# Third attention and late expert stages of a four-layer attention and expert network: first tiles, weight loads and the first group placed elsewhere

## The reference

```python
x = x + _L1_ffn_ref(_layernorm(x), ...)          # experts 1: top 2 of 8, capacity 256
# layer 2: 16 heads of 64, keys and values from the 128 context rows and the 128 latents
xn   = _layernorm(ctx, ln1_w, ln1_b);  latn = _layernorm(layernorm(x), ln2_w, ln2_b)
q, kv = latn @ Wq, concat([xn, latn]) @ Wkv
x = x + heads_attention(q, k, v) @ Wo
# experts 2 (top 2 of 8, gated, hidden 256); experts 3 (top 1 of 8, gelu, hidden 512)
hidden = silu(gate_out) * up_out;  expert_out = hidden @ down_w[e]
x = x + _L3_xattn_ref(...)                       # attention 3: one head of 128
h = gelu(x @ w1[e] + b1[e]);  y = h @ w2[e] + b2[e]
```

## Time and profile before

| what | us |
| --- | --- |
| median of 3 runs | 1901.37 |
| their range | 1900.53 to 1907.52 |
| profiled execution | 1909.33 |
| its span | 1907.6 |
| busy: PE, PEld, DVE, ACT, POOL | 1488.1, 1337.0, 1164.3, 824.9, 763.8 |
| mean granted TensorE clock | 0.852 of 2.4 GHz |

### The profile page before, as it was taken

How to read it: one execution, slowest core, us unless ns; L and a number is a source line. 1 busy time by engine, 2 the same in 40 slices (tenths; PEclk the granted TensorE clock), 3 DMA queues, 4 the chain that set the end, 5 groups by cost and what they waited for, 6 DMA issues and landing times. The chain is left out here.

```text
span 1907.6 us, 36653 instructions
## 1 busy us (share of the span) xinstructions
PE 1488.1 (78%) x10440; PEld 1337.0 (70%) x10441; DVE 1164.3 (61%) x3672; ACT 824.9 (43%) x2537; POOL 763.8 (40%) x757
## 2 busy tenths in 40 slices
PE   6776999425677639999999999999994898446394
PEld 4555899313466539999999999999993787224294
DVE  4556344217867337787778777777775455574244
ACT  4343455201222126666666666666661232313152
POOL 2011543560000535454747474756454355011442
PEclk8786899756666769999999999999997899766597
DMA  9002322110011230000000000000001522200223
GB/s 190 1 0 70 118 65 59 47 48 1 1 45 45 57 97 13 1 12 1 24 1 22 0 22 1 21 0 11 3 10 34 149 72 65 89 9 14 63 64 114
DMA packets 91845, 79.06 MB, mean 41 GB/s; under 512 B 16820, under 2 KB 78871, under 8 KB 91623
## 3 DMA queue, kind: packets, MB, share of 16 engines
q1 hardware_dynamic: 70712, 44.92, 9.0%
q0 software_dynamic: 11936, 24.52, 4.4%
q10 hardware_dynamic: 9104, 8.53, 1.5%
HBM read 51.36 MB, written 27.60 MB: 41 GB/s over the span
## 5 line engine op out<-in xcount | busy, mean ns | idle before, releaser
L1838 POOL TENSOR_TENSOR paired_rows<-paired_rows,rinv 128x1024 f32<-128x1024 f32 x128 | 242.3, 1893 | 284.6 <-DVE rinv L2123 281.6
L2002 ACT ACTIVATE paired_rows<-psum_banks,neg_max 128x256 f32<-128x256 f32 x512 | 237.4, 490 | 0.2
L2114 DVE TENSOR_TENSOR probs_turned_lo<-psum_banks,probs_turned_hi 128x512 fp32r<-128x512 f32 x256 | 175.5, 686 | 96.4 <-ACT probs_turned_hi L1984 82.8
L1888 PE MATMUL psum_banks<-y_turned_parts,queries_hi 128*128 128x256 f32 x1024 | 199.9, 293 | 3.0 <-DVEq L1739 3.0
L1923 PE MATMUL psum_banks<-probs_turned_hi,y_rows 128*128 128x512 f32 x512 | 192.0, 416 | 0.4 <-issue 0.4
L1984 ACT CAST probs_turned_hi<-psum_banks 128x512 fp32r<-128x512 f32 x256 | 151.1, 590 | 57.5 <-PE psum_banks L1872 55.1
L1872 PE MATMUL psum_banks<-ident,paired_rows 128*128 128x128 f32 x1024 | 154.9, 274 | 7.8 <-DVEq L1739 4.4
L1888 PEld LDWEIGHTS psum_banks<-y_turned_parts,queries_hi 128*128 128x128 f32 x1024 | 158.0, 191 | 3.5 <-issue 3.5
L2128 DVE TENSOR_REDUCE neg_max<-psum_banks 128x4 f32<-128x1024 f32 x128 | 155.9, 1218 | 6.5 <-PE psum_banks L1888 3.5
L1984 ACT CAST queries_hi<-psum_banks 128x512 fp32r<-128x512 f32 x128 | 75.0, 586 | 172.5 <-PE psum_banks L1911 167.6
L1888 PE MATMUL psum_banks<-y_turned_parts,queries_lo 128*128 128x256 f32 x512 | 144.5, 282 | 0.0
(11 more groups left out here) (717 smaller groups left out, 3386.2 us busy)
## 6 DMA issues: line engine op xcount, KB each, us to landing
tile_rows__<-rows_by_expert SPq DMA_DIRECT2D x71, 64.5 KB
expert_rows<-expert_rows_sb SPq DMA_DIRECT2D x71, 64.0 KB, 1.5
normed_rows_dram<-paired_rows SPq DMA_DIRECT2D x2, 2048.0 KB, 8.9
staged_pairs<-expert_rows SPq DMA_DIRECT2D x8, 512.0 KB
paired_rows<-expert_rows SPq DMA_DIRECT2D x8, 512.0 KB, 6.0
tile_rows___<-rows_by_expert SPq DMA_DIRECT2D x39, 64.5 KB
x_rows<-in_x_dram SPq DMA_DIRECT2D x8, 256.0 KB, 5.3
expert_w_b<-in_L_ffn_w_dram SPq DMA_DIRECT2D x1, 2048.0 KB
```

The source lines that it names most:

```text
L1838: ins = pool.tensor_tensor(probs[:, p, :, :], probs[:, p, :, :], rinv[:, p, :].unsqueeze(2).to_broadcast([P, 4, 256]), ALU.mult)
L1888: ins = pe.matmul(bank[S_BANKS[par] + h // 2][:, (h % 2) * 256:(h % 2 + 1) * 256], queries[q][:, h, :], yparts[:, 2 * s2 + y, :], start=(k ...
L2002: ins = act.activation(probs[:, par, h, :], bank[S_BANKS[par] + h // 2][:, (h % 2) * 256:(h % 2 + 1) * 256], ACT.Exp, bias=nmax[:, par, h: ...
L2114: ins = dve.tensor_tensor(lo, bank[bank_][:, :], hi.bitcast(F32), ALU.subtract)
```

## The change

**First group of the third attention.** GpSimd no longer adds the pairs of group 0 and no longer norms its rows; it only norms its context. VectorE adds the pairs (8 instructions), takes the statistics, ScalarE makes the inverse root by a logarithm and an exponential (`roots`, which was there for the last group), VectorE refines it once and norms the four tiles.

**Tiles ahead of the barrier.** `tile_rows` is now one tile of 8 slots of 129 columns for the whole program; the staged pairs lie in it. SP waits at the end of `attention_2` and `attention_3`, in GpSimd's place, until all rows are scattered, then for the tables, and issues the loads of tiles 0 and 1 of the next stage. `load_tile` in `experts` begins with tile 2.

**Weights of stage 3.** ScalarE issues them in `experts(2)` behind its part of step k = 1, that is behind four steps.

```diff
@@ experts @@
-                xr = sb_in(ph, "tile_rows", [P, SLOTS, P + 1 if kept else P])
+                xr = tile_rows
...
-                        for j in range(SLOTS):
+                        for j in range(AHEAD, SLOTS):
                             load_tile(j, j)
...
-                    if layer == 2:
-                        load_expert_weights(act, layer + 1)
+                        if layer == 2 and isinstance(k, int) and k == 1:
+                            load_expert_weights(act, layer + 1)
...
+        def load_rows(sp, layer, j, s, free):
+            at = sp.value_load(tile_base[0:1, bass.ds(j, 1)], min_val=0, max_val=E * REGION // P + SPARE_TILES - 1)
+            if not isinstance(j, int) or j >= SLOTS:
+                free()
...
+            sp.dma_start(tile_rows[:, s, :], src).then_inc(tile_loaded[s].sem, 16)
+
+        def load_first_tiles(sp, layer):
+            sp.wait_ge(tables_made.sem, tables_made.value + 1)
+            for j in range(AHEAD):
+                load_rows(sp, layer, j, j, None)
@@ attention_2 @@
-                staged = sb_in(ph, "staged_pairs", [P, G, 2, P])
+                staged = carve(flat(tile_rows[:, :, :]), 0, [P, 2 * G, P]).rearrange("p (j k) d -> p j k d", k=2)
...
                     sp.wait_ge(pads_placed.sem, 16 * E)
+                    sp.wait_ge(rows_spread.sem, 16 * 2 * G * NG)
+                    load_first_tiles(sp, 2)
...
-                    for c in range(10):
-                        norm_part(0, c)
+                    norm_context(0)
...
                     spread(NG - 1, range(2 * G))
-                    pool.wait_ge(rows_spread.sem, 16 * 2 * G * NG)
...
+                def roots(act, own, which):
+                    act.wait_ge(spread_known.sem, spread_known.value + which)
+                    act.activation(row_work[:, 2, own], row_work[:, 0, own], ACT.Ln, scale=-2.0)
+                    act.drain()
+                    act.activation(row_rstd[:, own], row_work[:, 2, own], ACT.Exp, scale=-0.5).then_inc(roots_made.sem, 1)
...
                     keep_turned(act, 0, Q_BANK, context_turned, 0, 2)
+                    roots(act, slice(0, 2 * G), 1)
                     keep_turned(act, 0, Z_BANK, latents_turned, P, 4)
...
-                    dve.wait_ge(pairs_combined.sem, 1)
+                    dve.wait_ge(pairs_staged.sem, 16)
+                    for k in range(2):
+                        for j in range(G):
+                            xt = x_tile(0)(j)
+                            ins = dve.scalar_tensor_tensor(xt, staged[:, j, k, :], WT[:, k, j:j + 1], xt, ALU.mult, ALU.add)
+                        ch.link()
+                    dve.sem_inc(pairs_combined.sem, 1)
                     row_stats(dve, ch, 0, 0)
                     aggregate(dve, ch, [0])
-                    seed(dve, ch)
-                    refine(dve, ch, 3)
-                    keep_scales(dve, ch, 0, None)
+                    dve.tensor_scalar(row_work[:, 0, :], row_mv[:, :, 1], -0.5 * (1.0 + EPS), -0.5 * EPS * EPS, ALU.mult, ALU.add).then_inc(spread_known.sem, 1)
+                    dve.wait_ge(roots_made.sem, roots_made.value + 1)
+                    refine(dve, ch, 1)
+                    for j in range(G):
+                        ins = dve.tensor_scalar(latents[:, j, :], x_tile(0)(j), row_mv[:, j, 0:1], row_rstd[:, j:j + 1], ALU.subtract, ALU.mult)
+                    ins.then_inc(latents_normed.sem, 1)
@@ attention_3 @@
                     sp.wait_ge(pads_placed.sem, 2 * 16 * E)
+                    sp.wait_ge(rows_spread.sem, 16 * (2 * B + B))
+                    load_first_tiles(sp, 3)
...
-                    pool.wait_ge(rows_spread.sem, 16 * (2 * B + B))
```

More of the change, by code:

```diff
@@ L38 @@
 SLOTS = 8
+AHEAD = 2
 RSQRT_SEED = 1597463007.0
@@ L164, in build @@
         row_number = sb("row_number", [P, B])
+        tile_rows = sb("tile_rows", [P, SLOTS, P + 1])
         spare_row = sb("spare_row", [P, TILES_TOP2])
@@ L185, in build @@
         first_weights = counter("first_weights")
+        tables_made = counter("tables_made")
         mask_words = counter("mask_words")
@@ L1116, in load_tile @@
                     def load_tile(j, s):
-                        at = sp.value_load(tile_base[0:1, bass.ds(j, 1)], min_val=0, max_val=E * REGION // P + SPARE_TILES - 1)
-                        if not isinstance(j, int) or j >= SLOTS:
-                            slot_is_free(sp, j, s)
-                        src = xb.rearrange("(t p) d -> t p d", p=P)[bass.ds(at, 1), :, :].rearrange("a p d -> (a p) d")
-                        sp.dma_start(xr[:, s, :], src).then_inc(arrived[s].sem, 16)
+                        load_rows(sp, layer, j, s, lambda: slot_is_free(sp, j, s))
                     if kept:
-                        for j in range(SLOTS):
+                        for j in range(AHEAD, SLOTS):
                             load_tile(j, j)
@@ L1151, in _ @@
                                 pool.wait_ge(rows_turned.sem, j + (rows_turned.value - SLOTS + 1))
-                            pool.indirect_dma_start(xr[:, j % SLOTS, :], None, xn, bass.IndirectOffsetOnAxis(ap=SOURCE[:, j:j + 1], axis=0)).then_inc(sorted_in[j % SLOTS].sem, 16)
+                            pool.indirect_dma_start(xr[:, j % SLOTS, 0:P], None, xn, bass.IndirectOffsetOnAxis(ap=SOURCE[:, j:j + 1], axis=0)).then_inc(sorted_in[j % SLOTS].sem, 16)
                         i = j - LAG
@@ L1615, in build @@
         KVT = SETB[:, 0:B * 2 * P].rearrange("p (b k) -> p b k", k=2 * P)
+        def load_rows(sp, layer, j, s, free):
+            at = sp.value_load(tile_base[0:1, bass.ds(j, 1)], min_val=0, max_val=E * REGION // P + SPARE_TILES - 1)
+            if not isinstance(j, int) or j >= SLOTS:
+                free()
+            src = xb.rearrange("(t p) d -> t p d", p=P)[bass.ds(at, 1), :, :].rearrange("a p d -> (a p) d")
+            sp.dma_start(tile_rows[:, s, :], src).then_inc(tile_loaded[s].sem, 16)
[3 more added lines that the diff above has]
+                load_rows(sp, layer, j, j, None)
         def tile_tables(dve, ch, n_tiles, ends, region, marks, scratch):
@@ L1635, in tile_tables @@
             ch.link(dve.tensor_reduce(jump, mark, AX.X, ALU.add))
-            dve.tensor_tensor(tile_base[:, 0:n_tiles], jump, number, ALU.add)
+            dve.tensor_tensor(tile_base[:, 0:n_tiles], jump, number, ALU.add).then_inc(tables_made.sem, 1)
         def place_pads(eng, experts_, turn):
@@ L2162, in _ @@
                     keep_turned(act, 0, Q_BANK, context_turned, 0, 2)
+                    roots(act, slice(0, 2 * G), 1)
                     keep_turned(act, 0, Z_BANK, latents_turned, P, 4)
                     all_steps(act_step)(act)
-                    act.wait_ge(spread_known.sem, spread_known.value + 1)
-                    act.activation(row_work[:, 2, G:2 * G], row_work[:, 0, G:2 * G], ACT.Ln, scale=-2.0)
-                    act.drain()
-                    act.activation(row_rstd[:, G:2 * G], row_work[:, 2, G:2 * G], ACT.Exp, scale=-0.5).then_inc(roots_made.sem, 1)
+                    roots(act, slice(G, 2 * G), 2)
                     keep_tail(act, NG - 1)
@@ L2179, in _ @@
                     ch.link(dve.tensor_copy(ends, region))
-                    dve.wait_ge(pairs_combined.sem, 1)
+                    dve.wait_ge(pairs_staged.sem, 16)
[5 more added lines that the diff above has]
+                    dve.sem_inc(pairs_combined.sem, 1)
                     row_stats(dve, ch, 0, 0)
                     aggregate(dve, ch, [0])
-                    seed(dve, ch)
-                    refine(dve, ch, 3)
-                    keep_scales(dve, ch, 0, None)
+                    dve.tensor_scalar(row_work[:, 0, :], row_mv[:, :, 1], -0.5 * (1.0 + EPS), -0.5 * EPS * EPS, ALU.mult, ALU.add).then_inc(spread_known.sem, 1)
[4 more added lines that the diff above has]
+                    ins.then_inc(latents_normed.sem, 1)
+                    dve.sem_inc(scales_made.sem, 1)
                     all_steps(lambda eng, i, c: dve_step(eng, ch, i, c))(dve)
@@ L2191, in _ @@
                     dve.tensor_scalar(row_work[:, 0, G:2 * G], row_mv[:, G:2 * G, 1], EPS, -0.5, ALU.add, ALU.mult).then_inc(spread_known.sem, 1)
-                    dve.wait_ge(roots_made.sem, roots_made.value + 1)
+                    dve.wait_ge(roots_made.sem, roots_made.value + 2)
                     refine(dve, ch, 1)
@@ L2207, in attention_2 @@
                 for c in (spread_known, roots_made):
-                    c.value += 1
+                    c.value += 2
+                tables_made.value += 1
                 for c in (PEs, ACs, D, SCALED):
```

## The result

| | before | after |
|---|---|---|
| median of 20 runs each, same chip | 1905.73 us | 1900.18 us |
| lowest to highest | 1899.0 to 1916.37 | 1893.9 to 1904.9 |
| ratio | | 0.9969, 95% interval 0.9955 to 0.9983 |
| profiled execution, span | 1907.6 us | 1895.5 us |

The change gains 5.9 us (1905.73 x 0.0031; 3.2 to 8.6 by the interval), where 12.0 were forecast. The two profiled executions differ by 12.1 us, but part of that lies in blocks that nothing changed: the first attention is 4 us longer after, the second 8 us shorter. Every ratio in this document leaves out runs in a slower state: one of the kernel before (2960.21 us) and one of e11 (1901.62 us).

The account below looks back on a forecast made before the run. TensorE was taken to bound the attention and experts bodies, so time saved before them counts. The terms 7.5 + 7.0 - 0.6 - 2.3 + 0.4 = 12.0 us, from 1901.4, gave 1889.4 us, range 1883 to 1899.

Parts of the forecast that it names:

- A: First group of the third attention: the new chain lets TensorE turn the normed rows earlier, 7.5 us gained.
- Rival 5: Group 0, third attention: pairs land later or the root waits behind the context; gain there 4, time 1892.9 us; chance 0.08.
- B: Start of experts(2): tiles 0 and 1 loaded ahead of the barrier let TensorE start earlier, 7.0 us gained.
- rival 3: Barriers: SP's loads lie fully in front, 2.1 us each, so only experts(3)-sized gains remain; 1893.7 us; chance 0.10.
- C: experts(2), step k = 1: issuing the weights on ScalarE makes gate 3 and tile 3's output late, 0.6 us lost.
- D: experts(2), first turn of the slots: tile 8's load meets the weights and TensorE waits, 2.3 us lost.
- E: Start of experts(3): early tiles help little because VectorE's first copy waits for b2, 0.4 us gained.
- rival 1: experts(2): streams alternate, so tile 8's load gets its turn at once and costs nothing; 1887.1 us; chance 0.22.
- Rival 2: experts(2): tile 8's load takes 7.31 us, TensorE waits 4.6, half clock costs 4.5; 1896.2 us; chance 0.15.
- Rival 4: experts(2): two slot turns stall in the weights and 8 tiles run at half clock; 1908.3 us, slower; chance 0.05.

Follow-up runs that it names:

- e11: Full change plus a third weight transfer of 2 MB behind the two at k = 1; 1.3 us faster than the kernel before, ratio 0.9993.
- e5: The full change run again, unaltered, beside the kernels of the second set; 7.3 us faster than the kernel before, ratio 0.9962.
- e1: Full change cut to the third attention's new first group: no tiles ahead, weights issued at start of experts(2); 6.5 us faster than before, ratio 0.9966.
- e2: Full change, but the weights are issued at the start of experts(2) again; 8.0 us faster than the kernel before, ratio 0.9958.
- e4: New first group, no tiles ahead of the barriers, experts(3) weights issued in the fourth attention; 11.3 us faster than the kernel before, ratio 0.9941.
- e3: Full change, but SP issues the 4 MB of experts(3) weights in the fourth attention; 11.3 us faster than the kernel before, ratio 0.9941.
- e9: As e7, but no tiles loaded ahead of the barriers, on the third set's chip; 17.2 us faster than the kernel before, ratio 0.9905.
- e10: Same kernel as e7, run on the third set's chip as partner of e9; 18.4 us faster than the kernel before, ratio 0.9898.
- e7: As e3, with b2 for experts(3) also loaded in the fourth attention, in its own buffer; 18.7 us faster than the kernel before, ratio 0.9902.
- e6: Full change, but only 2 MB of weights at k = 1, the other 2 MB in the fourth attention; 17.0 us faster than before, ratio 0.9911.
- e8: Full change, but the 4 MB of weights issued inside experts(2) in 16 pieces of 256 KB; 15.5 us faster than before, ratio 0.9919.

## Why the prediction was wrong

The forecast was 12.0 us of gain, and 5.9 came (7.3 in e5). Step by step:

- **A, first group, 7.5:** right. 7.5 by the profile, chain 6.50 for 6.44; e1, which has nothing else, gains 6.5 (4.2 to 8.6). Rival 5 falls.
- **B, early tiles, 7.0:** right at its place, 7.8 in the block less 0.49 for the barrier (last scatter to barrier 4.93 us, 4.44 before); rival 3 falls. Within the sets the barrier comes 0.8 to 1.2 us later with the early tiles than without (e1 and e2, e4 and e3, e9 and e10).
- **C, issue on ScalarE, 0.6:** tile 7 is turned 12.35 us behind tile 0, 11.46 before, which is 0.9; but 0.4 of it stands at tile 3 already, before the weights are issued, and e3 and e7, in which ScalarE issues nothing there, have 12.6 and 12.2. So C fits, and isn't shown.
- **D, the ring's first turn in the stream, 2.3: this is the step that failed**, mis-sized though its place was right. Tile 8 was turned 20.95 us behind tile 0 instead of 13.51, so 6.5 us went there beyond C's 0.9. Two assumptions failed. The scatter in front of the load was given no term of its own, since it lay in the weights' tail before; it took 6.4 us instead of 3.7 (2.1 to 2.3 without a stream), so even the upper bound of 4.6 us was too low. And the load was given the middle between 2.68 and 7.31 us, because it would come into a flowing stream; it took 7.0. The scatter costs 2.7 us, the load 4.3, and the scatter's later issue 0.4. Behind the wait comes what the clock costs: the gain lost is 8.7 us at tile 9, 9.2 at tile 10 and 8.2 at tile 12, so 0.8 to 1.8 us beyond the 7.4 of tile 8. Two tiles run at half clock.
- **E, experts(3), 0.4:** right that b2 takes the tiles' place: VectorE's copy is 0.3 us later behind the issue of b2 than before, the block is 95.27 us in e5 and 95.43 before, 93.96 in the other profile. e7 shows it from the other side.

With D and the clock as measured the sum is 7.5 + 7.3 - 0.9 - 7.3 + 0.4 = 7.0 us, within the interval of the 5.9.

The trace of the kernel before held the full price. By its landing times all eight tile loads issued at the start of experts(2) took 6.6 to 7.7 us, and not only that of tile 0. That tiles 2 to 7 never made TensorE wait, which the prediction counts for rival 1, came from their early issue.

Rival 2 comes nearest, with both its parts, a load at its full price and the clock behind it. That its 5.2 us stand so close to the 5.9 measured is in part luck: its wait of 4.6 us was about 2 too short, since it too left the scatter out, and its 4.5 for the clock about 3 too dear. Rival 1 falls with the wait of 6.70. The Trainium skill, "DMA: Bandwidth & Descriptors", "Queues, rings and completion order", says of the turns between queues that a DMA engine drains a whole packet of several descriptors from one ring before it goes to the next. In the trace, the first scatter's first packet moved 4.7 us after its issue (1.5 in e3), tile 8's 3.7 (1.0 in e3). So the small transfers do get their turn, and don't wait for all bytes ahead (e6), but late; whether the unit of the turn or something in front of the queues makes it late is not settled by a run. Rival 4 didn't happen at 4 MB; e11 got to no gain by another way.

Where the expected gain went is shown best by e5, e7 and e8 on one chip: the early tiles win 7.8 us at the block's start, and the stream, which was moved out of their way, takes it back 8 tiles later. Break the stream up (e8) or take it away (e7) and experts(2) is 7.0 and 7.8 us shorter, of which under 1 us lies behind tile 12. The first set agrees with smaller sizes: without the stream experts(2) is 3.1 us shorter with the early tiles (e3 against e2) and 4.7 without them (e4 against e1).

## What to carry to other kernels

Here a small transfer that met a long one paid a further 4 to 5 us, with 2 MB queued as with 4. Whether that holds for other sizes and queues wasn't measured. So count the transfers in a row that meet it (here scatter, then load, per turn of the ring), and put each at its full price. A prefetch of megabytes belongs in a block whose engines don't wait on small transfers (e3), or in pieces between them (e8); moving it by a few steps moves the stall (e2 against e5). And when a wait is removed, look for what the same engine gets next: b2 here, until it was loaded ahead too.

## What the runs showed of the hardware

- A scatter or load of 64 KB took mostly 2.1 to 2.3 and 1.6 to 2.0 us alone, 5.8 to 7.1 and 6.4 to 7.3 in the middle of a stream of 4 MB, and 6.6 (first scatter) and 7.0 (tile 7) in one of 2 MB. Next to pieces of 256 KB the scatters took 2.1 to 3.7 and the loads up to 2.5 (e8).
- The third large DMA issue in a row held ScalarE for 10.62 us (the first two 0.40 and 1.35). The Trainium skill, "DMA: Bandwidth & Descriptors", "Issuing engines are not separate DMA queues", calls the time on the issuer usually small relative to the DMA itself; here it was half of the 20.6 us from issue to landing.
- Chips differ: the kernel before took 1905.73, 1908.99 and 1912.06 us in three comparisons, and 1805.56 on the chip of the third set. There experts(2) took 123.26 us (e10) instead of 144.74 for the same kernel (e7), at a granted clock of 1.00 in the body of both. The third attention is about as long on both (788.88 and 790.68 us). Why is open.
